# Adding routed-expert rows by accumulating DMAs: gathers into resident tokens for 30 tiles, scatters into the output for 9

## The chip, the core and the metric

The kernel runs on one core of one Trainium2 chip. The metric is the device time of one execution in microseconds (us), lower is better. The engines that matter here are TensorE (PE, matmuls; PEld is its weight load), VectorE (DVE), ScalarE (ACT), GpSimd (POOL), which issues the indirect DMAs, and SyncE (SP), which issues most plain DMAs. They run unsynchronised and wait on semaphores; a DMA adds 16 to its semaphore when it has landed.

## The reference

A decoder block over x of 4 x 512 tokens, 256 wide: a state-space mixer, a cross-attention over 1601 context rows, and a mixture of 8 experts of which each token takes two. Only the last is touched by the change:

```python
x = x + mixer(layernorm(x))
x = x + cross_attention(layernorm(x), ctx, mask)
xt = layernorm(x)                                    # 2048 tokens x 256
scores = xt @ Wg.T                                   # 8 experts
topk_scores, topk_idx = top_k(scores, 2)
gate = silu(einsum('td,ehd->teh', xt, W1));  up = einsum('td,ehd->teh', xt, W2)
y = einsum('teh,edh->ted', gate * up, W3)            # hidden width 704
w = einsum('tke,tk->te', onehot(topk_idx), topk_scores)
out = x + einsum('te,ted->td', w, y)
```

## The kernel before

Two phases follow each other, each one block of five engine programs. `mixer_phase` computes mixer and attention; the residual stream `x_all` (16 groups of 128 tokens) stays in SBUF, and SP stores the normalised tokens to DRAM as `xn3_dram` (L306; the trace calls it `xn_dram`). At its start it also writes zeros over the DRAM tensor `ffn_sorted` (L270), with a source that lies in `yg`.

`routed_ffn_phase` sorts the token-expert pairs by expert. Each expert's pairs are padded to whole tiles of 128 rows, NT = 39 tiles in all. DVE's routing chain (L1278 to L1361) finds the two experts of each token, the place of each pair (`pos_f`, then `pos`: for each token its lower and its higher place), and, through one-hot tables and 32 small matmuls (L1447), the token of each place (`tok_id`). `first` and `w_low` put the two weights in the order of the places. POOL then gathers the 39 tiles of tokens from DRAM (L1180).

The tiles run in order of the experts. For tile i TensorE transposes the tokens, makes gate and up (`gate_up`, L1478), transposes the hidden rows (L1487, L1491) and multiplies by W3 (`down`, L1503); each product is three matmuls over a high and a low part of the operands. The steps are staggered: `gate_up` of tile i + 1 stands before `down` of tile i. DVE takes from each tile `rest_of_hidden`, `rest_of_tokens`, `multiply` and `evacuate` (L1388), which copies the result from PSUM to `y_sb`; SP stores it to `ffn_sorted` (L1109) and loads tokens of tile i + 4 into `tok_in` (L1104). POOL also loads and splits the weights of experts 2 to 7 (L1151, L1154).

The end: when the stores of all experts but the last are there, POOL gathers for each token its row at the lower place into `y_one`, 16 gathers (L1195); when all 39 tiles are stored, the 16 rows at the higher places, into the space of `tok`. DVE adds each with its weight (L1425, L1430) and SP stores two groups at a time to the output (L1132):

```python
for p in range(2):
    pool.wait_ge(y_st[p], so_far(NT - 1 if (NT - 1) % 2 == p else NT - 2, p))
fetch(y_two, 1, lambda g: up_ld[g // 2])
...
nc.vector.scalar_tensor_tensor(out=x_all[:, g, :], in0=y_two[:, g, :], scalar=w_low[:, 1, g:g + 1],
                               in1=x_all[:, g, :], op0=ALU.mult, op1=ALU.add).then_inc(comb, 1)
```

Of the kernel before, what the change touches and what calls it, by code (L numbers as in the profile page):

```python
# [17 lines left out]
NEG_HUGE = -3.0e38  # L18


def at(i, n=1):
    return bass.ds(i, n)
# [9 lines left out]
def decoder_kernel(nc, io, dims):  # L32
    B, S, D, S2, DI, NST, TAPS, E, HF = dims
    KD = D // P
    KI = DI // P
    T = S // P
    G = B * T
    KC = -(-S2 // P)
    S2_LAST = S2 - (KC - 1) * P
    CH = -(-S2 // 4)  # L40
    CHUNKS = [(c * CH, min(S2, (c + 1) * CH)) for c in range(4)]
    KH = -(-HF // P)
    H_LAST = HF - (KH - 1) * P
    HH = HF // 2
    NT = (2 * B * S + E * (P - 1)) // P

    ffn_sorted = nc.dram_tensor("ffn_sorted", [NT * P, D], F32).ap()
    xn3_dram = nc.dram_tensor("xn3_dram", [G * P, D], F32).ap()
# [42 lines left out]
def mixer_phase(nc, io, dims, env, sem, buf):  # L91
# [9 lines left out]
    xn3_dram, b_dram, NT = (env[k] for k in ("xn3_dram", "b_dram", "NT"))  # L101
# [7 lines left out]
    with ExitStack() as ctx:  # L109
# [3 lines left out]
        def ps(name):  # L113
# [50 lines left out]
        zeros, ones, bo_row = yg[:, 0, 0:D], yg[:, 1, 0:P], yg[0:1, 2, 0:D]  # L164
# [12 lines left out]
            sem(n) for n in ("x_ld", "xr_ld", "wi_ld", "w_ld", "wa_ld", "b_st", "b_ld", "ctx_ld", "mask_ld", "tok_st", "res_st"))  # L177

# [70 lines left out]
        with nc.Block() as block:  # L249

            @block.sync
            def _(sp):
# [5 lines left out]
                for dst, src in (  # L258
# [44 lines left out]
                def store_tokens(b):  # L303
                    for t in range(T):
                        sp.wait_ge(LN[2]["xn"], b * T + t + 1)
                        sp.dma_start(xn3_dram[at(b * S + t * P, P), :], xn[:, t, :]).then_inc(tok_st, 16)  # L306
# [7 lines left out]
                for b in range(B):  # L314

                    if b >= 1:
                        load_mask(b - 1, 2)
                        load_mask(b - 1, 3)
                    if b + 1 < B:
                        store_b(b + 1)  # L320
                        load_b(b + 1, 0)
                        load_b(b + 1, 1)
                    if b >= 1:
                        context(b)
                        load_mask(b, 0)
                        load_mask(b, 1)
                    if b + 1 < B:
                        load_b(b + 1, 2)
                        load_b(b + 1, 3)
                    if b >= 1:  # L330
                        store_tokens(b - 1)
                load_mask(B - 1, 2)
# [209 lines left out]
            def _(dve):  # L542
# [42 lines left out]
                def read_out(b, j):  # L585
# [5 lines left out]
                    if isinstance(b, int) and b == 0 and j == 0:  # L591
                        dve.wait_ge(res_st, 16)
                        dve.wait_ge(res_st, 16)
# [372 lines left out]
def routed_ffn_phase(nc, io, dims, env, sem, buf):  # L966
# [5 lines left out]
    KD, G, KH, H_LAST, HH, NT = (env[k] for k in ("KD", "G", "KH", "H_LAST", "HH", "NT"))  # L972
# [8 lines left out]
    with ExitStack() as ctx:  # L981
# [8 lines left out]
        tok = sb("tok", [P, NT, D])  # L990
# [21 lines left out]
        first = sb("first", [P, 2, G])  # L1012
        w_low = sb("w_low", [P, 2, G])
# [19 lines left out]
        y_one = sb("y_one", [P, G, D])  # L1033
        y_two = tok[:, 0:G, :]

# [35 lines left out]
        low_ld, up_ld, comb = sem("low_ld"), [sem(f"up_ld{g}") for g in range(G // 2)], sem("comb")  # L1071
# [21 lines left out]
        with nc.Block() as block:  # L1093

            @block.sync
            def _(sp):
# [3 lines left out]
                def load(i, q):  # L1100

                    come = gathered(i) if isinstance(i, int) else (i - q) * (16 // PAIRS) + 32
                    sp.wait_ge(tok_ld[q // 2], come)
                    sp.dma_start(tok_in[:, q % 2, :], tok[:, at(i), :].rearrange("p a d -> p (a d)")  # L1104
                                 ).then_inc(tile_ld[q % 2], 16)
# [15 lines left out]
                LAST = (NT - AHEAD) // GROUP * GROUP  # L1121
# [14 lines left out]
            def _(pool):  # L1136
                nc.gpsimd.iota(iot[:], pattern=[[1, P]], base=0, channel_multiplier=0).then_inc(iota_ok, 1)
                nc.gpsimd.iota(num[:], pattern=[[P, G]], base=0, channel_multiplier=1).then_inc(iota_ok, 1)
# [4 lines left out]
                nc.gpsimd.memset(seg[:, :, 0:1], 0.0).then_inc(one_ok, 1)  # L1143

# [48 lines left out]
                def fetch(y, k, done):  # L1193
                    for g in range(G):
                        pool.indirect_dma_start(y[:, g, :], None, ffn_sorted,  # L1195
                                                bass.IndirectOffsetOnAxis(ap=pos[:, k, g:g + 1], axis=0)).then_inc(done(g), 16)
# [63 lines left out]
            def _(dve):  # L1260
# [59 lines left out]
                chain(nc.vector.tensor_tensor(first[:, 0, :], pos_f[:, 0, :], pos_f[:, 1, :], ALU.is_lt))  # L1320
                chain(nc.vector.tensor_scalar(first[:, 1, :], first[:, 0, :], -1.0, 1.0, ALU.mult, ALU.add))
# [3 lines left out]
                nc.vector.tensor_copy(pos[:], pos_f[:]).then_inc(pos_ok2, 1)  # L1325


# [75 lines left out]
                def pair(i):  # L1403
                    for k in range(2):
                        rest_of_hidden(i + k - 1)
                        rest_of_tokens(i + k + 1, k)
                        multiply(i + k, 1 - k)
                        evacuate(i + k - 1, k)

                pair(1)  # L1410
                with dve.Fori(3, NT - 2, 2) as i:
                    pair(i)
                rest_of_hidden(NT - 3)
                rest_of_tokens(NT - 1, 0)
                multiply(NT - 2, 1)
                evacuate(NT - 3, 0)
                rest_of_hidden(NT - 2)
                multiply(NT - 1, 0)
                evacuate(NT - 2, 1)
                rest_of_hidden(NT - 1)  # L1420
                evacuate(NT - 1, 0)

                dve.wait_ge(low_ld, 16 * G)
                for g in range(G):
                    nc.vector.scalar_tensor_tensor(out=x_all[:, g, :], in0=y_one[:, g, :], scalar=w_low[:, 0, g:g + 1],  # L1425
                                                   in1=x_all[:, g, :], op0=ALU.mult, op1=ALU.add).then_inc(comb, 1)
                for g in range(G):
                    dve.wait_ge(comb, g + 1)
                    dve.wait_ge(up_ld[g // 2], 32)
                    nc.vector.scalar_tensor_tensor(out=x_all[:, g, :], in0=y_two[:, g, :], scalar=w_low[:, 1, g:g + 1],  # L1430
                                                   in1=x_all[:, g, :], op0=ALU.mult, op1=ALU.add).then_inc(comb, 1)
# [150 lines left out]
```

## Time and profile before

| what | value |
|---|---|
| median of 3 runs | 1149.94 us |
| the runs | 1152.03, 1149.91, 1149.94 us |
| the profiled execution, first to last instruction | 1151.0 us |
| mean granted TensorE clock, as a share of full speed | 0.885 |
| busy share of PE, PEld, DVE, ACT, POOL | 81%, 64%, 58%, 39%, 51% |

The profile is of one execution. Its own device time is not listed apart from its span of 1151.0 us, which lies between the lowest and the highest of the runs. The second phase begins at 788.94 us of the span. A row of the timeline gives start, duration, engine, line, operation, what it writes and reads, and in brackets how long its engine was idle before and what ended that. A row of the chain of waits gives start, duration and what the chain went through.

### The profile page before, as it was taken

What the parts mean: (1) busy time and instruction counts of PE and PEld (TensorE: products, weight loads), DVE (VectorE), ACT (ScalarE), POOL (GpSimd) and SP (SyncE); (2) the same over time, 40 slices, a digit from 0 to 9 for tenths busy, and PEclk for the clock granted to TensorE, in tenths of its full rate; (3) what the DMA queues carried; (4) which work ended last, traced back from release to release, by engine and by line L of the source; (5) the groups of instructions that cost most, each with busy time, mean ns of one, the idle gap of its engine ahead of it and who ended that gap; (6) DMA issues with size and microseconds to landing.
All of it is one profiled execution on the core that took longest, in us unless ns stands there. A gap on an engine that the chain in (4) does not pass through costs nothing. (4 is left out here: it accounts for less than half of the span.)

```text
span 1151.0 us, 16215 instructions
## 1 busy us (share of the span) xinstructions
PE 928.8 (81%) x5148; PEld 731.9 (64%) x5149; DVE 669.2 (58%) x1097; ACT 445.6 (39%) x827; POOL 590.9 (51%) x481
## 2 busy tenths in 40 slices
PE   5767677889877889885989877992699999999970
PEld 2344345457666546665657765672689899999970
DVE  4189777697457788547677872416634343443443
ACT  2455754355544445635345530322222222222210
POOL 2176675755446565546576743110578553335505
PEclk9869877899886899996899987995699999999995
DMA  9440030000044000026000040004365312311304
GB/s 322 161 175 1 1 111 37 1 15 1 1 163 132 1 9 7 1 75 220 1 8 8 1 147 1 15 1 169 123 207 127 125 48 100 112 36 36 109 19 146
DMA packets 48954, 85.44 MB, mean 74 GB/s; under 512 B 6292, under 2 KB 38696, under 8 KB 46856
## 3 DMA queue, kind: packets, MB, share of 16 engines
q1 hardware_dynamic: 43032, 65.77, 17.0%
q0 software_dynamic: 5872, 19.02, 5.7%
q8 instruction: 29, 0.48, 0.2%
q14 instruction: 21, 0.17, 0.0%
HBM read 65.64 MB, written 14.55 MB: 70 GB/s over the span
## 5 line engine op out<-in xcount | busy, mean ns | idle before, releaser
L373 POOL TENSOR_TENSOR u<-dtx,b_all 128x512 f32<-128x512 f32 x256 | 326.6, 1288 | 212.9 <-DVE h L620 209.7
L620 DVE TENSOR_TENSOR_SCAN h<-da,u 128x512 f32<-128x512 f32 x256 | 308.6, 1217 | 136.8 <-ACT da L455 89.5
L455 ACT ACTIVATE da<-dt_,a_neg 128x512 f32<-128x512 f32 x256 | 174.8, 689 | 133.3 <-DVE h L620 132.5
L746 PE MATMUL ysum<-ident,h 128*128 128x128 f32 x1024 | 159.3, 301 | 57.9 <-DVE h L620 44.5
L746 PEld LDWEIGHTS ysum<-ident,h 128*128 128x128 f32 x1024 | 132.5, 156 | 104.2 <-DVE h L620 56.8
L924 PE MATMUL pv<-pT,ctx_n 128*128 128x128 f32 (+1 forms) x832 | 109.5, 288 | 7.6 <-DVE x_all L681 7.6
L924 PEld LDWEIGHTS pv<-pT,ctx_n 128*128 128x128 f32 (+1 forms) x832 | 104.6, 204 | 10.8 <-DVE x_all L681 9.1
L895 PE MATMUL pa<-ctx_t,xnT_a 128*128 128x401 f32 (+1 forms) x256 | 97.3, 508 | 13.9 <-DVE sim L602 12.6
L1367 DVE TENSOR_TENSOR hid<-act_,ps_u 128x352 f32<-128x352 f32 x78 | 40.6, 521 | 86.8 <-ACT act_ L1221 86.8
L1221 ACT ACTIVATE act_<-ps_g 128x352 f32<-128x352 f32 x78 | 36.3, 466 | 104.2 <-PE ps_u L1478 104.2
L1503 PE MATMUL ps_y<-w_hi,hidT_hi 128*128 x234 | 70.9, 303 | 2.7 <-DVE hidT_lo L1381 2.7
L895 PEld LDWEIGHTS pa<-ctx_t,xnT_a 128*128 128x128 f32 x256 | 44.9, 192 | 44.2 <-DVE sim L602 19.2
L729 PE MATMUL pm<-xnT_m,w_in 128*128 128x512 f32 x128 | 65.1, 637 | 6.3 <-DVE xs L576 4.8
L1503 PE MATMUL ps_y<-w_lo,hidT_hi 128*128 x234 | 66.5, 284 | 0.0
L1503 PE MATMUL ps_y<-w_hi,hidT_lo 128*128 x234 | 66.3, 283 | 0.0
L1226 ACT CAST hidT_hi<-ps_h 128x512 fp32r<-128x512 f32 x39 | 22.9, 586 | 104.3 <-PE ps_h L1491 100.1
L1180 POOL DMA_INDIRECT tok<-xn_dram,tok_id x39 | 43.9, 1125 | 35.3 <-DVE tok_id L1349 23.7
L1381 DVE TENSOR_TENSOR hidT_lo<-ps_h,hidT_hi 128x512 fp32r<-128x512 f32 (+2 forms) x117 | 42.1, 415 | 34.1 <-ACT hidT_hi L1226 34.1
L602 DVE COPY_PREDICATED sim<-mask,pa 128x401 f32<-128x401 uint8 x64 | 38.0, 596 | 37.1 <-PE pa L895 37.1
L1154 POOL TENSOR_TENSOR w_lo<-w_raw,w_hi 128x2816 fp32r<-128x2816 f32 (+1 forms) x12 | 58.6, 4882 | 0.0
L1478 PE MATMUL ps_g<-w_hi,tokT_hi 128*128 x156 | 54.6, 350 | 3.4 <-issue 3.3
L1162 POOL TENSOR_TENSOR pool_scrap<-ident 128x1 f32<-128x1 f32 x26 | 4.8, 193 | 96.3 <-PE ps_y L1503 85.3
(216 smaller groups left out, 1780.5 us busy)
## 6 DMA issues: line engine op xcount, KB each, us to landing
b_all<-b_dram SPq DMA_DIRECT2D x16, 1024.0 KB, 4.6
ctx_t<-in_ctxT SPq DMA_DIRECT2D x4, 1601.0 KB
ctx_n<-in_ctx SPq DMA_DIRECT2D x4, 1536.0 KB
ffn_sorted<-yg SPq DMA_DIRECT2D x1, 4992.0 KB, 22.5
ffn_sorted<-y_sb SPq DMA_DIRECT2D x39, 128.0 KB
tok_in<-tok SPq DMA_DIRECT2D x35, 128.0 KB, 2.0
mask<-in_mask SPq DMA_DIRECT2D x16, 200.1 KB, 2.4
w_raw<-in_w1T SPq DMA_DIRECT2D x4, 704.0 KB, 4.2
```

The source lines that it names most:

```text
L373: nc.gpsimd.tensor_tensor(u[:, i % 2, :], dtx[:, j % 2, :], b_all[:, n, :], ALU.mult).then_inc(u_ok, 1)
L455: nc.scalar.activation(da[i % DS][:], dt_[:, j % 2, :], ACT.Exp, scale=a_neg[:, j, n:n + 1]).then_inc(da_ok, 1)
L620: nc.vector.tensor_tensor_scan(h[:, i % HS, :], da[i % DS][:], u[:, i % 2, :], 0.0, ALU.mult, ALU.add).then_inc(scan_ok, 1)
L729: last = nc.tensor.matmul(bank[:], w_in[:, k, j * P:(j + 1) * P], xnT_m[:, k, :], start=k == 0, stop=k == KD - 1)
L746: last = nc.tensor.matmul(ysum[:, t * P:(t + 1) * P], h[:, i % HS, t * P:(t + 1) * P], ident[:], is_transpose=True, start=n == 0 and t == ...
L895: last = nc.tensor.matmul(pa[c % 2][:, 0:hi - lo], xnT_a[:, k, q * P:(q + 1) * P], ctx_t[:, k, lo:hi], start=k == 0, stop=k == KD - 1)
L924: last = nc.tensor.matmul(pv[:, k * P:(k + 1) * P], ctx_n[0:w, c, k * P:(k + 1) * P], pT[0:w, c, :], start=c == 0 and k == 0, stop=c == KC ...
L1154: nc.gpsimd.tensor_tensor(w_lo[:, p * NW + lo:p * NW + hi], w_raw[:, p, lo:hi], w_hi[:, p * NW + lo:p * NW + hi].bitcast(F32), ALU.subtrac ...
L1180: pool.indirect_dma_start(tok[:, i, :], None, xn3_dram, bass.IndirectOffsetOnAxis(ap=tok_id[:, i:i + 1], axis=0)).then_inc(tok_ld[i // 2 % ...
L1381: nc.vector.tensor_tensor(hidT_lo[0:rows_in, c:c + n, :], bank[0:rows_in, col:col + n * P].rearrange("p (c m) -> p c m", m=P), hidT_hi[0:r ...
L1478: last = nc.tensor.matmul(out[:, 0:HH], x[:, p, k * P:(k + 1) * P], w[:, at(e % 2 * NW + (first + k * HF), HH)], start=k == 0 and n == 0, ...
L1503: last = nc.tensor.matmul(ps_y[:, 0:D], x[0:rows_in, c, :], w[0:rows_in, at(e % 2 * NW + (2 * NGU + c * D), D)], start=c == 0 and n == 0, ...
```

## The change

A row's weight is applied when its tile is evacuated. For that the scores travel with the tokens: `xn3_dram` and `tok` have rows of 256 + 8 numbers, row 0 of `xn3_dram` is zero and belongs to empty places, and four stores write the scores. From them DVE works out one weight per row of each tile (`tile_masks`, `row_weights`).

The results of tiles 0 to 29 go to `ffn_sorted` as before. When tile 29 is stored, POOL adds them to `x_all` with 32 gathers that accumulate in SBUF; a place in a later tile points at a row of zeros. SP then stores `x_all` to the output. The results of tiles 30 to 38 stay in SBUF (`y_late`), and after SP's stores POOL adds them to the output in DRAM with 17 scatters that accumulate: 8 for rows that are their token's lower place, 9 for the higher, with waits between, so that no two additions to a row are in flight together. Rows that a scatter is not to add go to spare rows behind the output (`late_rows` works out where). The DVE additions at the end, `y_one`, `first` and `w_low` are gone. DVE's loop over pairs of tiles is written out.

```diff
-                sp.dma_start(env["ffn_sorted"].rearrange("(n p) d -> p n d", p=P),
-                             zeros.unsqueeze(1).to_broadcast([P, NT, D])).then_inc(res_st, 16)
+                sp.dma_start(env["ffn_sorted"][EARLY * P:(EARLY + 1) * P, :], zeros[:, 0:D]).then_inc(res_st, 16)
+                sp.dma_start(xn3_dram[0:1, :], zeros[0:1, :]).then_inc(res_st, 16)
...
+                def store_scores(b):
+                    sp.wait_ge(r_ok, b + 1)
+                    sp.dma_start(xn3_dram[at(b * S + 1, S), D:D + E].rearrange("(t p) e -> p t e", p=P),
+                                 scores[:, b * T:(b + 1) * T, :]).then_inc(score_st, 16)
...
+                store_scores(B - 1)
                 sp.wait_ge(tok_st, 16 * B * T)
+                sp.wait_ge(score_st, 16 * B)
...
+        BATCHES = [range(LATE - 3)] + [range(t, t + 1) for t in range(LATE - 3, LATE - 1)]
...
-                for i in range(LAST, NT - AHEAD):
+                for i in range(LAST, EARLY):
                     store_and_load(i, i % GROUP)
-                for i in range(NT - AHEAD, NT):
-                    store(i, i % 2)
-                out = io["out"].rearrange("(g p) d -> p g d", p=P)
+                for i in range(EARLY, NT - AHEAD):
+                    sp.wait_ge(y_ok2, i + 1)
+                    load(i + AHEAD, (i + AHEAD) % GROUP)
+                out = io["out"][0:G * P, :].rearrange("(g p) d -> p g d", p=P)
                 for g in range(0, G, 2):
-                    sp.wait_ge(comb, G + g + 2)
+                    sp.wait_ge(both_ld[g // 2], 64)
                     sp.dma_start(out[:, g:g + 2, :], x_all[:, g:g + 2, :]).then_inc(out_st, 16)
...
+                nc.gpsimd.memset(above[:], 1.0).then_inc(above_one, 1)
+                pool.wait_ge(above_one, 1)
+                nc.gpsimd.memset(above[:, :, E:E + 1], 0.0).then_inc(above_one, 1)
...
+                def add_early(k, g):
+                    pool.indirect_dma_start(x_all[:, g, :], None, ffn_sorted,
+                                            bass.IndirectOffsetOnAxis(ap=pos[:, k, g:g + 1], axis=0),
+                                            compute_op=ALU.add).then_inc(both_ld[g // 2], 16)
+
+                def add_late(k, t, done):
+                    pool.wait_ge(y_ok2, EARLY + t + 1)
+                    pool.indirect_dma_start(io["out"], bass.IndirectOffsetOnAxis(ap=late_to[:, k, t:t + 1], axis=0),
+                                            y_late[:, t, :], None, compute_op=ALU.add).then_inc(done, 16)
...
                 for p in range(2):
-                    stores = pool.value_load(tile_end[0:1, E + p:E + p + 1], min_val=1, max_val=NT)
-                    pool.wait_ge(y_st[p], stores * 16)
-                    take_wait()
-                fetch(y_one, 0, lambda g: low_ld)
-
-                for p in range(2):
-                    pool.wait_ge(y_st[p], so_far(NT - 1 if (NT - 1) % 2 == p else NT - 2, p))
-                fetch(y_two, 1, lambda g: up_ld[g // 2])
+                    pool.wait_ge(y_st[p], so_far(EARLY - 1 if (EARLY - 1) % 2 == p else EARLY - 2, p))
+                for g in range(G):
+                    add_early(0, g)
+                for g in range(G):
+                    pool.wait_ge(both_ld[g // 2], 32)
+                    add_early(1, g)
+
+                pool.wait_ge(late_ok, 1)
+                pool.wait_ge(out_st, 16 * (G // 2))
+                for n, batch in enumerate(BATCHES):
+                    for t in batch:
+                        add_late(0, t, low_st[n])
+                    if n == 0:
+                        pool.wait_ge(low_st[0], 16 * len(BATCHES[0]))
+                    else:
+                        pool.wait_ge(low_st[n - 1], 16 * len(BATCHES[n - 1]))
+                    for t in batch:
+                        add_late(1, t, high_st)
+                pool.wait_ge(low_st[len(BATCHES) - 1], 16)
+                add_late(1, LATE - 1, high_st)
+                pool.wait_ge(high_st, 16 * LATE)
...
-                chain(nc.vector.tensor_tensor(first[:, 0, :], pos_f[:, 0, :], pos_f[:, 1, :], ALU.is_lt))
-                chain(nc.vector.tensor_scalar(first[:, 1, :], first[:, 0, :], -1.0, 1.0, ALU.mult, ALU.add))
...
-                nc.vector.tensor_copy(pos[:], pos_f[:]).then_inc(pos_ok2, 1)
...
                 for k in range(2):
-                    chain(nc.vector.tensor_tensor(w_part[:, 0, :], w_top[:, 0, :], first[:, k, :], ALU.mult))
-                    chain(nc.vector.tensor_tensor(w_part[:, 1, :], w_top[:, 1, :], first[:, 1 - k, :], ALU.mult))
-                    chain(nc.vector.tensor_tensor(w_low[:, k, :], w_part[:, 0, :], w_part[:, 1, :], ALU.add))
+                    chain(nc.vector.tensor_scalar(is_late[:, k, :], pos_f[:, k, :], float(EARLY * P), None, ALU.is_ge))
+                    chain(nc.vector.tensor_scalar(to_zero[:, k, :], pos_f[:, k, :], num_f[:, 0:1], float(EARLY * P - 1),
+                                                  ALU.subtract, ALU.subtract))
+                    chain(nc.vector.tensor_tensor(to_zero[:, k, :], to_zero[:, k, :], is_late[:, k, :], ALU.mult))
+                    chain(nc.vector.tensor_tensor(pos_f[:, k, :], pos_f[:, k, :], to_zero[:, k, :], ALU.subtract))
+                nc.vector.tensor_copy(pos[:], pos_f[:]).then_inc(pos_ok2, 1)
...
                 def evacuate(i, p):
                     dve.wait_ge(y_mm, i + 1)
-                    wait(dve, y_st[p], so_far(i - 2, p))
-                    nc.vector.tensor_copy(y_sb[:, p, :], ps_y[:, 0:D]).then_inc(y_ok2, 1)
+                    if i < EARLY:
+                        wait(dve, y_st[p], so_far(i - 2, p))
+                    y = y_sb[:, p, :] if i < EARLY else y_late[:, i - EARLY, :]
+                    nc.vector.tensor_scalar(y, ps_y[:, 0:D], w_row[:, i:i + 1], None, ALU.mult).then_inc(y_ok2, 1)
...
+                rest_of_hidden(0)
+                rest_of_tokens(2, 0)
+                multiply(1, 1)
+                tile_masks()
+                row_weights(0, KNOWN)
+                for i in range(NT):
+                    if i > 0:
+                        rest_of_hidden(i)
+                        if i + 2 < NT:
+                            rest_of_tokens(i + 2, i % 2)
+                        if i + 1 < NT:
+                            multiply(i + 1, (i + 1) % 2)
+                    if i == KNOWN:
+                        row_weights(KNOWN, NT)
+                    if i == KNOWN + 1:
+                        late_rows()
+                    evacuate(i, i % 2)
```

`KNOWN` is 8. `tile_masks` is two DVE operations, `row_weights` two with a wait for the gathers of its tiles, and `late_rows` some twenty, on at most 9 x 8 numbers a partition.

## Rows read from the trace of the kernel before

**Rows 1.** The page: the span, and busy tenths of PE in 40 slices.
```profile
span 1151.0 us, 16215 instructions
PE   5767677889877889885989877992699999999970
```
**Rows 2.** The chain of waits, from the last tile's matmuls to the end.
```profile
1114.36 3.92 PE ps_y L1503 x18
...
1118.31 0.44 DVE y_sb L1388
...
1120.72 1.22 POOL tok L1195
...
1142.60 2.85 DMA tok<-ffn_sorted,pos
```
**Rows 3.** Timeline of POOL: last weight split, last lower gather, second higher gather.
```profile
1050.88 3.51 POOL L1154 TENSOR_TENSOR w_lo<-w_raw,w_hi 128x1536 fp32r<-128x1536 f32 x1
...
1084.33 0.96 POOL L1195 DMA_INDIRECT y_one<-ffn_sorted,pos  x1 [0.30 <-issue]
...
1122.24 3.65 POOL L1195 DMA_INDIRECT tok<-ffn_sorted,pos  x1 [0.30 <-issue]
```
**Rows 4.** The chain of waits: `down` of tiles 29 and 35.
```profile
1051.90 2.34 PE ps_y L1503 x18
...
1095.02 2.34 PE ps_y L1503 x18
```
**Rows 5.** Timeline of POOL: plain loads of 640 rows and of 64.
```profile
885.65 0.91 POOL L1079 DMA_DIRECT2D w_raw<-in_w3T  x1
886.52 0.63 POOL L1081 DMA_DIRECT2D w_raw<-in_w3T  x1
```
**Rows 6.** DMA queues from 1064 to 1086 us, POOL's: packets, MB, share of 16 engines.
```profile
q0 software_dynamic: 721, 1.97, 32.7%
```
**Rows 7.** DMA issues: count, KB each, median us from issue to landing.
```profile
out<-x_all SPq DMA_DIRECT2D x8, 256.0 KB, 2.3
...
xn_dram<-xn SPq DMA_DIRECT2D x16, 128.0 KB, 3.9
...
b_dram<-sp_pos SPq DMA_DIRECT2D x4, 32.0 KB, 1.6
```
**Rows 8.** Timeline of DVE at the end: the lower additions, the last higher pair.
```profile
1118.65 6.41 DVE L1425 SCALAR_TENSOR_TENSOR x_all<-y_one,w_low,x_all 128x256 f32<-128x256 f32 x16
...
1145.54 0.88 DVE L1430 SCALAR_TENSOR_TENSOR x_all<-tok,w_low,x_all 128x256 f32<-128x256 f32 x2 [1.66 <-DMA tok<-ffn_sorted,pos]
```
**Rows 9.** Token gathers as one group (min/median/max ns, first to last start); DVE beside them.
```profile
L1180 POOL DMA_INDIRECT tok<-xn_dram,tok_id x39: 956/960/4835, 813.9 to 868.4; - x39
...
815.90 4.74 DVE L1394 TENSOR_TENSOR w_lo<-w_raw,w_hi 128x2816 fp32r<-128x2816 f32 x2
```
**Rows 10.** Timeline where the phases meet; then the rank matmuls.
```profile
788.47 0.19 DVE L692 COPY scores<-pv 128x32 f32<-128x32 f32 x1 [5.68 <-PE pv L942]
788.94 0.38 SPq L1077 DMA_DIRECT2D w_raw<-in_w1T  x1
...
789.86 0.35 POOL L1146 TENSOR_SCALAR_AFFINE_SELECT tri<-tri 128x128 f32<-128x128 f32 x1
...
794.89 0.80 PE ps_g L1439 x2
```
**Rows 11.** The chain of waits: a routing step, the second half of the table matmuls.
```profile
800.93 0.19 DVE first L1320
...
809.77 3.59 PE ps_y L1447 x16
```
**Rows 12.** Timeline of DVE: evacuations of tile 0 and of a late tile.
```profile
838.34 0.42 DVE L1388 COPY y_sb<-ps_y 128x256 f32<-128x256 f32 x1 [1.76 <-PE ps_y L1503]
...
1083.13 0.42 DVE L1388 COPY y_sb<-ps_y 128x256 f32<-128x256 f32 x1 [1.44 <-PE ps_y L1503]
```
**Rows 13.** Timeline near the start: the clearing store, TensorE's wait for a load.
```profile
11.40 3.55 SPq L270 DMA_DIRECT2D ffn_sorted<-yg  x1
11.94 0.50 PEld L729 LDWEIGHTS pm<-xnT_m,w_in 128*128 128x128 f32 x2 [1.18 <-DMA b_conv<-in_b_conv]
```

More of the change, by code:

```diff
@@ L18 @@
 NEG_HUGE = -3.0e38
+OUT_OF_WAY = 1.0e30
+LATE = 9
 def at(i, n=1):
@@ L100, in mixer_phase @@
     x_all, ident, scores = env["x_all"], env["ident"], env["scores"]
-    xn3_dram, b_dram, NT = (env[k] for k in ("xn3_dram", "b_dram", "NT"))
+    xn3_dram, b_dram, EARLY = (env[k] for k in ("xn3_dram", "b_dram", "EARLY"))
     STEPS = KI * NST
@@ L163, in mixer_phase @@
         b_qkv = sb("b_qkv", [P, 3, KD])
-        zeros, ones, bo_row = yg[:, 0, 0:D], yg[:, 1, 0:P], yg[0:1, 2, 0:D]
+        zeros, ones, bo_row = yg[:, 0, 0:D + E], yg[:, 1, 0:P], yg[0:1, 2, 0:D]
         ysum = ps("ysum")
@@ L331, in _ @@
                         store_tokens(b - 1)
+                        store_scores(b - 1)
                 load_mask(B - 1, 2)
@@ L1032, in routed_ffn_phase @@
         tile_expert = sb("tile_expert", [1, LOOP], I32)
-        y_one = sb("y_one", [P, G, D])
-        y_two = tok[:, 0:G, :]
+        y_late = sb("y_late", [P, LATE, D])
+        above = sb("above", [P, NT, E + 1])
+        w_tile = sb("w_tile", [P, NT, E])
+        w_row = sb("w_row", [P, NT])
+        low_s = sb("low_s", [P, LATE, E])
+        high_s = sb("high_s", [P, LATE, E])
+        low_max = sb("low_max", [P, LATE])
+        high_max = sb("high_max", [P, LATE])
+        row_id = sb("row_id", [P, LATE])
+        taken_by = sb("taken_by", [P, 2, LATE])
+        dump = sb("dump", [P, 2, LATE])
+        away = sb("away", [P, 2, LATE])
+        late_to = sb("late_to", [P, 2, LATE], U32)
+        is_late = sb("is_late", [P, 2, G])
+        to_zero = sb("to_zero", [P, 2, G])
         place_row = w_lo[:, NW:NW + 2 * G * P].rearrange("p (k g m) -> p k g m", k=2, g=G)
@@ L1070, in routed_ffn_phase @@
                              "y_ok2"))
-        low_ld, up_ld, comb = sem("low_ld"), [sem(f"up_ld{g}") for g in range(G // 2)], sem("comb")
+        both_ld = [sem(f"both_ld{g}") for g in range(G // 2)]
+        above_one, w_row_ok, late_ok = sem("above_one"), sem("w_row_ok"), sem("late_ok")
+        BATCHES = [range(LATE - 3)] + [range(t, t + 1) for t in range(LATE - 3, LATE - 1)]
+        low_st, high_st = [sem(f"low_st{n}") for n in range(len(BATCHES))], sem("high_st")
+        KNOWN = 8
         def load_expert(eng, e, p, done):
@@ new lines, in row_weights, with late_rows @@
+                def row_weights(lo, hi):
+                    for n in range(PAIRS):
+                        last = max(i for i in range(hi) if i // 2 % PAIRS == n)
+                        dve.wait_ge(tok_ld[n], gathered(last))
+                    chain(nc.vector.tensor_tensor(w_tile[:, lo:hi, :], w_tile[:, lo:hi, :], tok[:, lo:hi, D:D + E], ALU.mult))
+                    chain(nc.vector.reduce_sum(w_row[:, lo:hi], w_tile[:, lo:hi, :], AX_X))
+                def late_rows():
+                    own, late = tok[:, EARLY:NT, D:D + E], above[:, EARLY:NT, :]
+                    chain(nc.vector.tensor_scalar(low_s[:], late[:, :, 1:E + 1], OUT_OF_WAY, -OUT_OF_WAY, ALU.mult, ALU.add))
+                    chain(nc.vector.tensor_tensor(low_s[:], low_s[:], own, ALU.add))
+                    chain(nc.vector.scalar_tensor_tensor(out=high_s[:], in0=late[:, :, 0:E], scalar=-OUT_OF_WAY, in1=own,
+                                                         op0=ALU.mult, op1=ALU.add))
+                    chain(nc.vector.reduce_max(low_max[:], low_s[:], AX_X))
+                    chain(nc.vector.reduce_max(high_max[:], high_s[:], AX_X))
+                    chain(nc.vector.tensor_copy(row_id[:], tok_id[:, EARLY:NT]))
+                    chain(nc.vector.tensor_scalar(taken_by[:, 0, :], row_id[:], 1.0, None, ALU.is_ge))
+                    chain(nc.vector.tensor_tensor(taken_by[:, 1, :], low_max[:], high_max[:], ALU.is_ge))
+                    chain(nc.vector.tensor_tensor(taken_by[:, 1, :], taken_by[:, 1, :], taken_by[:, 0, :], ALU.mult))
+                    chain(nc.vector.tensor_tensor(taken_by[:, 0, :], taken_by[:, 0, :], taken_by[:, 1, :], ALU.subtract))
+                    for k in range(2):
+                        chain(nc.vector.tensor_scalar(dump[:, k, :], num_f[:, 0:LATE], float((G + k * LATE) * P - 1), None, ALU.add))
+                        chain(nc.vector.scalar_tensor_tensor(out=away[:, k, :], in0=row_id[:], scalar=-1.0, in1=dump[:, k, :],
+                                                             op0=ALU.add, op1=ALU.subtract))
+                    chain(nc.vector.tensor_tensor(away[:], away[:], taken_by[:], ALU.mult))
+                    chain(nc.vector.tensor_tensor(away[:], away[:], dump[:], ALU.add))
+                    nc.vector.tensor_copy(late_to[:], away[:]).then_inc(late_ok, 1)
@@ L1401, in _ @@
                 split_rest(1)
[L1403 to L1431, printed above, removed]
+                rest_of_hidden(0)
[15 more added lines that the diff above has]
+                    evacuate(i, i % 2)
             @block.tensor
```

37 lines of the change are left out of this document (19 added, 18 removed).

## The prediction

> **What bounds the kernel now.** I read the page first: TensorE (PE) is busy nine tenths or more in every slice from the 30th to the 38th, then 7 and 0 [rows 1]. So the end is set by two things in turn, TensorE and what follows it. The chain of waits shows them: the matmuls of the last tile end at 1118.28 us, DVE evacuates them, SP stores them, POOL wakes at 1120.72 and issues sixteen gathers, the last at 1142.60, which lands 2.85 later [rows 2]. VectorE (DVE) adds the last pair, SyncE (SP) stores it: the tail is 1151.0 - 1118.3 = 32.7 us in which TensorE does nothing. The timeline of POOL shows what is idle before: the last expert's split ends at 1054.4, the last of the 16 gathers of the lower rows ends at 1085.3, beside the matmuls, and then POOL waits until 1120.72 [rows 2, 3]. One gather follows the other in 0.96 busy + 0.30 = 1.26 us. Six tiles lie between the two `down` groups of [rows 4], 43.12 us, so a tile takes TensorE 7.19; they are those of tile 29, which ends at 1054.24, and of tile 35, at 1097.36.
>
> **The tail, part by part.** The change takes away the wait for all tiles before the second set, the 32 DVE additions, and the output stores at the end. It adds 17 accumulating scatters (8 lower tiles, 9 higher), so POOL has 32 + 17 = 49 indirect DMAs on one chain in place of 32, of which 16 lay beside matmuls. No row shows an accumulating DMA. Its issue is bounded below by the plain one, 1.26 us from start to start, and above by twice the busy time, 2 x 0.96 + 0.30 = 2.22 us, if every row needs all of its descriptor work twice. Between them, plain DMAs of POOL show what more rows cost: 0.63 us with 64 rows, 0.91 with 640 [rows 5], so 0.28/576 = 0.5 ns a row, 0.07 us for 128 more rows. An accumulating DMA reads one more row per row, so I take 1.26 + 0.07 = 1.33 us. On the DMA engines the 16 gathers of rows 3 took 32.7% of the engines over 22 us, 0.45 us each [rows 6]; with a second read twice that, 0.90 us, which is under 1.33 and so hides behind the issue, but I add 0.5 us to each landing that the chain waits for: 2.85 + 0.5 = 3.35 us.
>
> The Trainium skill (Collectives: The Full Stack, section The bandwidth ceiling) says that an add in a DMA is slow not for the add but because it reads two sources, with two read descriptors per chunk on one ring, about half the rate. That agrees with the doubling that I used for the transfer, 0.90 us; read as a rule for the issue too, it would give the 2.22 us of the first rival.
>
> The chain then, in times of the trace before:
> - POOL starts 2.44 us after tile 29's matmuls, as it did after tile 38's (1118.28 to 1120.72) [rows 2]: 1056.7. It is free of the split by 1054.4 [rows 3].
> - 31 starts of 1.33: 1097.9; landing 3.35: 1101.3. The waits for the lower rows of a pair cost nothing: they landed some 15 issues before.
> - SP stores the last pair, 2.3 us [rows 7]: 1103.7 with 0.1 of hand-over; POOL wakes after 0.3: 1104.0. SP's queue has the loads of tiles up to 38 ahead of these stores, the last of them after tile 34's evacuation at 1090.6; the stores of the first pairs stand behind it, but the last pair comes 10 us later, so 0.
> - Six lower scatters, last start after 5 x 1.33: 1110.6; landing 3.35 and 0.3: 1114.3. Tile 35 was ready at 1098.
> - Six higher, lower 6, higher 6, then lower 7 starts at + 8 x 1.33 (counted from the first higher): 1124.9; it lands and POOL wakes: 1128.6; the last scatter lands at 1131.9.
> - From the last landing to the end of the span before: the last output store starts after the DVE pair that ends at 1146.42, lands 2.3 later, at 1148.7, and 2.3 us remain [rows 7, 8]. So 1134.2.
>
> The last tile's rows are there at 1118.3 + 0.5 and are asked for at 1128.6: TensorE has 9 us of slack against POOL in the new order. In this chain 31 + 5 + 8 = 44 issue times count.
>
> DVE's 16 additions, back to back from 1118.65 for 6.41 us, also go. Beside them POOL's second gather took 3.65 us instead of 0.96 [rows 3, 8], and the longest token gather took 4.83 us beside DVE's two-input subtractions of 4.74 [rows 9]. This stall is in the old tail alone; next to the short DVE work of the tiles the 16 gathers stayed at 0.96, so I add none.
>
> **The start of the second phase.** The mixer's last act is now a store of the last scores. The scores are copied at 788.47 + 0.19, and the next phase began at 788.94 [rows 10], with no DMA between. Now SP waits for 512 pieces of 32 bytes: a 32 KB store took 1.6 us to land, the token stores 3.9 [rows 7]; I take 2.2, since these bytes are few but the pieces small. The score stores of the other three batches stand in SP's queue behind the token stores of their batch and ahead of the mask loads of the next, which wait for later attention steps: 0.
>
> The Trainium skill (DMA: Bandwidth & Descriptors, Specifications) says that under 512 bytes a transfer becomes a read-modify-write; no row here shows it. By that rule the upper end would be the nearer.
>
> In the routing chain the two `first` steps and the conversion of `pos`, 0.2 us each with their hand-over, go from ahead of the one-hot tables: -0.6. Behind the tables, six weight steps go and nine small ones come, 9 x 0.2 = 1.9 us; TensorE's 16 matmuls of 3.59 us cover them, as nothing waits for DVE before they end [rows 11]. Without that cover they would cost 1.9. POOL's two more memsets lie ahead of the triangle, which is ready at 790.2 and needed at 794.89 [rows 10]: 0, even at the 0.35 us of the triangle's own operation each. The gathers carry 1056 bytes for 1024, 3% of 0.45 us under an issue of 1.26: 0. Sum of this part: +2.2 - 0.6 = +1.6 (bounds +1.0 and +3.3).
>
> **Inside the tiles.** The weighted evacuation is one operation from PSUM for another, 0.42 us [rows 12]: 0. The two mask steps and the first two weight steps, four times 0.2 to 0.4, lie between multiply 1 and evacuation 0, where DVE waited 1.76 us. The second weight steps wait for all 39 gathers: the last started at 868.42 [rows 9], and tile 8 is evacuated 8 x 7.19 us after tile 0 (838.34), near 896. `late_rows`, some 20 steps of 0.2 = 4 us, comes before evacuation 9: DVE has 1.44 us of idle there [rows 12] and more behind it, 7.19 us a tile against some 3.5 of work, so the tile absorbs most; 0, at worst 2.5, and even that lies in the 9 us of slack, save for tile 29, from which POOL starts. DVE's tile loop is now written out; if its code comes late, it eats the same 1.44 us.
>
> **The start of the kernel.** The 4992 KB clearing store is cut to 128 KB. The only wait of TensorE for a load near it, 1.18 us for `b_conv`, ended at 11.94, half a microsecond after that store was issued, so it was due to earlier transfers [rows 13]: 0, at most -1.2.
>
> **Sum.** 1134.2 + 1.6 = 1135.8 against a span of 1151.0: -15.2 us. The median of the runs is 1149.94, 1.1 under that span, so 1134.7; I say 1135.
>
> **Rivals.**
> - The plain price holds: 1.26 us and a landing of 2.85. Then 44 x 0.07 + 4 x 0.5 = 5.1 us less: 1129.6. The 16 gathers beside the matmuls speak for it; that they read one source speaks against. It belongs to the forecast's own case, as does an issue up to 1.60 (+12: 1147).
> - The accumulating issue costs POOL twice: 2.22 us. Then 44 x 0.89 = 39 us more: 1174, slower. It decides from 1.33 + 15.2/44 = 1.68 us on, a busy time of 1.38 against 0.96. For it: the indirect DMA's 0.96 against 0.63 for a plain one says that work per row matters. Against it: 0.5 ns a row for the plain ones.
> - The DMA engines become the bound: read, read and write of a row in sequence, four times 0.45 = 1.8 us per DMA. The rings fill and the chain goes at 1.8: 44 x 0.47 = 21 us more, 1156, slower. For it: 1 KB rows; against: the gathers of rows 6 kept the engines busy for only a third of the time.
> - The change does not help because POOL's chain is simply moved: the start of the adds waits for something later than tile 29. Each tile of delay costs 7.2 us, so two give 1149, no change. No row speaks for it; the stores and the split end before.
>
> **How the numbers follow.** Forecast with an issue of 1.26 to 1.60: 0.68, its own range 1129 to 1147. POOL twice: 0.14. DMA engines: 0.11. Delayed start: 0.07. The range must leave out no more than 2 in 10: it goes from 1128 to 1158, which takes in the second slower case, and leaves out the first. This measurement can tell about 0.2%, 2.3 us. Faster: 0.68 and half of the delayed start, 0.71; same: 0.04; slower: 0.25.
>
> **What the profile after would show.** POOL's busy time for one accumulating DMA (0.96, 1.03 or 1.9) is the first thing to read; then the start of the first (1058), the start of the first scatter (1105), the last (1130), and TensorE's last matmul at 1118.3 + 1.6 = 1119.9. Wrong would be: a busy time above 1.38, landings beyond 5 us, or a second phase that begins later than 793.

## The result and the profile after

The changed kernel takes 1165.12 us (median of 4 runs, 1163.73 to 1167.2) against 1149.93 for the kernel before: ratio 1.013, 95% interval 1.0114 to 1.0147. It is 15 us slower where 15 us less were forecast. The profiled execution, the run of 1163.73, spans 1162.0 us.

The chain of waits of the changed kernel, its last part (answers to rows 2):

```profile
1113.09 1.56 POOL x_all L1224
1114.64 5.56 issue
1120.20 1.60 POOL out L1230
...
1129.57 3.76 DMA out<-y_late,late_to
1133.33 0.45 issue
1133.78 1.55 POOL out L1230
...
1148.63 3.75 DMA out<-y_late,late_to
1152.38 0.27 issue
1152.64 1.55 POOL out L1230
```

The whole end is now POOL and its landings. The gap of 5.56 us is the landing of the last gather, SP's last output store and its landing. TensorE has ended long before; the timeline of DVE shows the evacuation of its last tile, which starts 37 us ahead of the last scatter:

```profile
1115.63 0.48 DVE L1435 TENSOR_SCALAR y_late<-ps_y,w_row 128x256 f32<-128x256 f32 x1 [3.98 <-PE ps_y L1573]
```

The two kinds of accumulating DMA of the changed kernel, grouped by the tile they write (duration in ns min/median/max, first and last start, us); the plain one before took 0.96 us [rows 3]:

```profile
L1224 POOL DMA_INDIRECT x_all<-ffn_sorted,pos x32: 1548/1557/1712, 1055.2 to 1113.1; - x32
```
```profile
L1230 POOL DMA_INDIRECT out<-y_late,late_to x17: 1551/1552/1599, 1120.2 to 1152.6; - x17
```

The first gather, in the timeline of POOL, where the chain of the additions begins:

```profile
1055.19 1.71 POOL L1224 DMA_INDIRECT x_all<-ffn_sorted,pos  x1 [2.96 <-DMA ffn_sorted<-y_sb]
```

Busy 1.56 and 0.30 to the next make 1.86 us from start to start. The starts give (1113.09 - 1055.19)/31 = 1.87, as a few gathers took up to 1.71. On the DMA engines, from 1056 to 1114 us, POOL's queue (packets, MB, share of 16 engines) took 49.9% of 58 us for 31 gathers, 0.93 us each, where plain ones took 0.45 [rows 6]:

```profile
q0 software_dynamic: 4377, 3.99, 49.9%
```

So the transfer is twice as costly, as assumed, and hidden: POOL starts a gather every 1.87 us. What was put too low is the time of POOL itself. At the phases' border (timeline, answers to rows 10) SP now waits for its store of the scores:

```profile
787.68 0.19 DVE L703 COPY scores<-pv 128x32 f32<-128x32 f32 x1 [5.68 <-PE pv L953]
787.90 0.37 SPq L314 DMA_DIRECT2D xn_dram<-scores  x1
790.13 0.38 SPq L1102 DMA_DIRECT2D w_raw<-in_w1T  x1
```

From the end of the copy, 787.87, to the next phase it is 2.26 us; before it was 0.28.

### The profile page after: what moved, and what is told of

It reads as the page before. It is cut to its first block and busy times, and to the rows that moved or that the text cites. A ratio compares the mean times of both kernels' runs of the same rounds, so it can differ in the third digit from the quotient of the medians.

```text
span 1162.0 us, 15965 instructions
## 1 busy us (share of the span) xinstructions
PE 925.7 (80%) x5148; PEld 727.0 (63%) x5149; DVE 668.0 (57%) x1088; ACT 445.6 (38%) x827; POOL 634.3 (55%) x498
## 5 line engine op out<-in xcount | busy, mean ns | idle before, releaser
L740 PE MATMUL pm<-xnT_m,w_in 128*128 128x512 f32 x128 | 67.9, 660 | 6.4 <-DVE xs L588 4.3
L1209 POOL DMA_INDIRECT tok<-xn_dram,tok_id x39 | 44.3, 1136 | 34.5 <-DVE tok_id L1394 22.9
L1224 POOL DMA_INDIRECT x_all<-ffn_sorted,pos x32 | 50.0, 1562 | 12.4 <-issue 9.5
```

The source lines that it names most:

```text
L740: last = nc.tensor.matmul(bank[:], w_in[:, k, j * P:(j + 1) * P], xnT_m[:, k, :], start=k == 0, stop=k == KD - 1)
L1209: pool.indirect_dma_start(tok[:, i, :], None, xn3_dram, bass.IndirectOffsetOnAxis(ap=tok_id[:, i:i + 1], axis=0)).then_inc(tok_ld[i // 2 % ...
L1224: pool.indirect_dma_start(x_all[:, g, :], None, ffn_sorted, bass.IndirectOffsetOnAxis(ap=pos[:, k, g:g + 1], axis=0), compute_op=ALU.add). ...
```

## The experiments

Twelve kernels ran, in three groups; each group has its own runs of the kernel before beside it (median 1151.22, 1150.85 and 1151.93 us), and ratios are to those. e1 to e4 and e10 leave out or misplace part of the additions, so their output is not the reference's; e2, e3 and e10 ran once each, and are read by their traces.

**Is it the accumulating form, and of which DMAs?** In e1 the early gathers lose `compute_op`, in e4 the scatters do:

```diff
-                                            bass.IndirectOffsetOnAxis(ap=pos[:, k, g:g + 1], axis=0),
-                                            compute_op=ALU.add).then_inc(both_ld[g // 2], 16)
+                                            bass.IndirectOffsetOnAxis(ap=pos[:, k, g:g + 1], axis=0)).then_inc(both_ld[g // 2], 16)
```

> The 32 early gathers do not accumulate: they overwrite x_all, so the added rows replace the residual and the output is not the reference's. Theory A (accumulating costs POOL more for every DMA, 1.86 us from start to start in place of 1.26): the gathers go back to 1.26 us, the chain from the first gather to the out store is 31 x 0.60 = 18.6 us shorter and the landing about 1 us, so about 1145.5 us. Rival (the extra 27 us against the forecast lie mostly in waits and at the end, not in the issue): less than 10 us shorter, above 1155.

> The 17 late scatters overwrite the output rows instead of adding (the output is not the reference's). Theory A: their busy time goes from 1.55 to 0.96 us, 16 issues on the chain are 9.6 us shorter, the landings they wait for about 1 us each: about 1153 us. Rival: a scatter into DRAM costs more than a gather whether it adds or not, busy stays above 1.3: above 1160.

e1: 1147.34 us, ratio 0.9961 (0.9946 to 0.9975), 18 us under the changed kernel. e4: 1154.41 us, ratio 1.0035 (1.0021 to 1.0049), 11 us under it. The groups by tile, of e1:

```profile
L1224 POOL DMA_INDIRECT x_all<-ffn_sorted,pos x32: 945/949/1039, 1058.0 to 1097.0; - x32
```

and of e4:

```profile
L1230 POOL DMA_INDIRECT out<-y_late,late_to x17: 956/961/1048, 1122.8 to 1144.9; - x17
```

Gather or scatter, the plain form costs 0.95 to 0.96 us and the accumulating one 1.55 to 1.56. A scatter into DRAM is not dearer in itself, so e4's rival falls, and so does e1's. Together the two account for some 29 us, the shorter landings included: twice the loss.

**POOL's work or the DMA engines?** e2 halves the bytes of a row (first diff), e3 the rows (second):

```diff
-                    pool.indirect_dma_start(x_all[:, g, :], None, ffn_sorted,
+                    pool.indirect_dma_start(x_all[:, g, 0:D // 2], None, ffn_sorted.rearrange("n (h d) -> (n h) d", h=2),
```
```diff
-                    pool.indirect_dma_start(x_all[:, g, :], None, ffn_sorted,
-                                            bass.IndirectOffsetOnAxis(ap=pos[:, k, g:g + 1], axis=0),
+                    pool.indirect_dma_start(x_all[0:P // 2, g, :], None, ffn_sorted,
+                                            bass.IndirectOffsetOnAxis(ap=pos[0:P // 2, k, g:g + 1], axis=0),
```

> The 32 early accumulating gathers move 512 bytes a row in place of 1024, of other rows, 128 rows as before (the output is not the reference's). Theory A (POOL's work goes by rows): busy time stays at 1.55 us, the time at about 1165. Rival B (the DMA engines, which read two sources and write one, are the bound and hold POOL back): busy time falls clearly, towards 0.96, and the time by up to 18 us.

> The 32 early accumulating gathers take 64 rows in place of 128, of 1024 bytes (half of the tokens get no early rows). Theory A with all of the time per row: busy 0.78 us. Theory A with a fixed part like the 0.57 us at which a plain POOL DMA of 64 rows starts: busy 1.0 to 1.1 us. Rival B (bytes on the DMA engines): the same as in the run with half the bytes and all rows.

The gathers of e2, then of e3, grouped as above:

```profile
L1224 POOL DMA_INDIRECT x_all<-ffn_sorted,pos x32: 1548/1557/1711, 1057.1 to 1115.0; - x32
```
```profile
L1224 POOL DMA_INDIRECT x_all<-ffn_sorted,pos x32: 1419/1428/1591, 1055.1 to 1109.0; - x32
```

Half the bytes change nothing, 1.557 us; the time is 1164.74. On the DMA engines they did change something. POOL's queue, e2 from 1056 to 1110 us:

```profile
q0 software_dynamic: 3917, 1.79, 27.7%
```

That is 0.53 us for each of some 28 gathers in place of 0.93. So the DMA engines do not hold POOL back. Half the rows take 1.428 (e3, 1160.67 us), so a row costs 129/64 = 2.0 ns. If the time is a straight line over the rows, 1.30 us do not depend on them: more than either busy time that I had given for all of e3's DMA (0.78, 1.0 to 1.1). e10 halves the rows of e1's plain gathers (1146.12 us):

> The 32 early gathers plain and with 64 rows in place of 128 (output not the reference's). The accumulating gather took 1.56 us with 128 rows and 1.43 with 64: 2 ns a row and 1.30 us fixed. If the plain one has the same price per row, its busy time is 0.95 - 0.13 = 0.82 us and the accumulating form's extra 0.6 us is a fixed charge per DMA; if it has less than 1 ns a row (above 0.89), part of the extra goes by rows.

```profile
L1224 POOL DMA_INDIRECT x_all<-ffn_sorted,pos x32: 887/892/983, 1056.9 to 1094.1; - x32
```

A row of the plain form costs (949 - 892)/64 = 0.9 ns, and its fixed part, by the same straight line, is 0.83 us. Of the 0.61 us that accumulating adds per DMA of 128 rows, some 0.47 are fixed and 0.14 go by rows. The lines are drawn through two points each; no third number of rows was tried.

The queue also counts packets, and here the two forms differ. Divided by the bytes of one gather (128 KB, in e2 and e3 64 KB), a plain one has 48 packets (721 for 1.97 MB [rows 6]), an accumulating one 144 (4377 for 3.99 MB), and e2's, with all rows and half the bytes, 143. With 64 rows the accumulating one has 80; POOL's queue in e3, from 1056 to 1110 us:

```profile
q0 software_dynamic: 2468, 2.03, 27.6%
```

From 64 to 128 rows that is one packet a row for the accumulating form, and the plain one puts several rows into a packet. It may be why a row costs POOL more; that was not tried. It does not explain the fixed part: with 80 packets the accumulating DMA still takes 1.43 us, with 48 the plain one 0.95. What POOL does in these 0.47 us stays open.

**What follows the last landing.** In the changed kernel the last scatter starts at 1152.64 and lands some 3.8 later, at 1156.4; 5.6 us remain to the end of the span, where the kernel before had 2.3. e6 moves one line, from the end of POOL's program to the end of SP's:

```diff
+                sp.wait_ge(high_st, 16 * LATE)
...
-                pool.wait_ge(high_st, 16 * LATE)
```

> The changed kernel, but SP and not POOL waits for the landing of the last scatters. After the last landing (about 1156.4) the changed kernel still runs 5.6 us, the kernel before 2.3 us after its last landing. Theory C (POOL is slow to close its program after it has waited for its own DMA): POOL's closing then runs beside the landing, and the end comes 3 us sooner, about 1162 us. Rival D (the end of the block, or POOL's queue of DMAs, takes that long after the last accumulating scatter whoever waits): no change, 1165.

The scatters of e6, and the first line of its page:

```profile
L1231 POOL DMA_INDIRECT out<-y_late,late_to x17: 1550/1552/1599, 1123.9 to 1156.3; - x17
```
```profile
span 1163.2 us, 15965 instructions
```

From the last start to the end it is 6.9 us in place of 9.4, 2.5 us less: in the trace, part of what POOL still did after the landing now lies beside it. The time does not show it: 1164.88 us, ratio 1.0131 (1.0106 to 1.0156). In this execution the scatters began 3.7 us later than in the changed kernel's, for a part of the program that e6 does not touch. A gain of 2.5 us is within the interval, so whether the time gains it stays open, and with it rival D for the time.

**The parts that were costed at little.** e8 is the kernel before with the four score stores alone, e9 the kernel before with the clearing store cut to 8 tiles, e7 the kernel before with its lower additions (L1425), unchanged, moved between the steps of the last three tiles:

```diff
+                def add_low(groups):
+                    dve.wait_ge(low_ld, 16 * G)
+                    for g in groups:
...
                 evacuate(NT - 3, 0)
+                add_low(range(0, 5))
                 rest_of_hidden(NT - 2)
                 multiply(NT - 1, 0)
+                add_low(range(5, 8))
                 evacuate(NT - 2, 1)
+                add_low(range(8, 12))
                 rest_of_hidden(NT - 1)
+                add_low(range(12, 16))
                 evacuate(NT - 1, 0)
```

> The kernel before, with the four score stores of the change alone (to a DRAM tensor that nobody reads). The changed kernel's second phase began 2.26 us after SP issued the last of them was possible, in place of 0.28. Theory: +2.0 us, ratio 1.0017. Rival (the gap at the phases' border is hidden by POOL's and ScalarE's set-up): no change.

> The kernel before, with the clearing store cut from 39 tiles to the last 8 (4992 to 1024 KB). My forecast costed it at nothing: ratio 1.000. Rival: the changed kernel's first phase ended 0.8 us earlier (787.68 against 788.47), so the smaller store gives 0.8 us, ratio 0.9993.

> The kernel before, with the 16 additions of the lower rows moved from the end into the last three tiles of DVE's loop, nothing else. Theory E (DVE's additions back to back hold POOL's descriptor writing up: its second gather took 3.65 us instead of 0.96): the tail is 2.7 us shorter, ratio 0.9977. Rival (the second gather is slow for another reason, such as the first use after a pause): no change.

e8: ratio 1.0021 (1.001 to 1.0032), 2.4 us, near the 2.0 of its theory. e9: 0.9997 (0.9983 to 1.0011), which can't tell nothing from the 0.8 us of its rival. But the 0.8 us are no sign of the store: e9's own scores were copied at 789.12, later than the 788.47 before, and with the changed kernel's first phase the copy came anywhere from 786.69 (e4) to 789.15 (e6). e7: 1148.65 us, 0.9983 (0.9969 to 0.9996), 2 us faster. Its higher gathers, timeline of POOL:

```profile
1121.98 0.95 POOL L1195 DMA_INDIRECT tok<-ffn_sorted,pos  x1 [36.00 <-DMA ffn_sorted<-y_sb]
1123.23 0.95 POOL L1195 DMA_INDIRECT tok<-ffn_sorted,pos  x1 [0.30 <-issue]
```

The second takes 0.95 us where it took 3.65 [rows 3]: with the additions gone from beside it the delay is gone, and the pause ahead of the first gather, 36 us, is still there. So it was DVE's run of additions that held it, not a first use after a pause.

**Can the idea be had without the price?** h1 keeps the split at tile 30 and the scatters, but gathers plainly and lets DVE add, two groups at a time between the steps of tiles 31 to 36:

```diff
+        y_one, y_two = tok[:, G:2 * G, 0:D], tok[:, 0:G, 0:D]
...
+                def add_pair():
...
+                        nc.vector.tensor_tensor(x_all[:, g, :], x_all[:, g, :], (y_one, y_two)[k][:, g, :],
+                                                ALU.add).then_inc(comb, 1)
...
+                ADDS = {(EARLY + 1 + n // 3, n % 3) for n in range(G)}
```

> The changed kernel with its 32 early gathers plain, into the token buffer that is free by then, and the additions on DVE, two at a time, spread over the steps of tiles 31 to 36; the 17 scatters stay. Theory A (the price is the accumulating form's 0.60 us per DMA on POOL, and DVE has room): the first scatter starts at about 1101.4 in place of 1120.2, 18.8 us sooner: about 1146 us, ratio 0.9967. Rival F (32 more DVE additions delay TensorE or hold POOL's gathers up, as the 16 back to back did in the kernel before): first scatter after 1106, ratio 1.00 or more.

h1: 1148.38 us, ratio 0.9983 (0.9967 to 0.9998). The first scatter started at 1102.4, 17.8 us sooner than in the changed kernel, and the last tile was evacuated at 1115.9 against 1115.6 there, so rival F did not come. h2 has the scatters in another order, and DVE waits for four gathers at a time in place of two:

```diff
+ORDER = "L0 L1 L2 L3 L4 L5 H0 H1 H2 H3 L6 L7 H4 H5 H6 H7 H8"
...
+                        if t > 0:
+                            pool.wait_ge(low_st[t - 1], 16)
+                        add_late(1, t, high_st)
```

> The run before with the scatters in an order in which each finds the lower ones that it must follow landed: L0 to L5, H0 to H3, L6, L7, H4 to H8 (L lower, H higher, by late tile), each H waiting for one landing only. The waits of 2.66 and 0.30 us between the scatters go: 3 us less, about 1143 us, ratio 0.994. Rival G (landings of scatters to DRAM queue behind each other, so the waits come back at the H scatters): less than 1 us.

h2: 1147.79 us, 0.9972 (0.9959 to 0.9985). The first scatter started at 1103.8. The scatters of h2, grouped:

```profile
L1233 POOL DMA_INDIRECT out<-y_late,late_to x17: 1541/1548/1642, 1103.8 to 1133.5; - x17
```

29.7 us for 16 distances, 1.86 each: no wait is left in between, so rival G falls in the trace; the step in time, 0.6 us in the medians, is smaller than the 3 expected and inside both intervals. h3 changes several things at once: 5 tiles are scattered in place of 9, the lower gathers start when all experts but the last are stored, the additions lie in tiles 33 to 37, and SP waits for the last landing:

```diff
-LATE = 9
+LATE = 5
+ORDER = "L0 L1 H0 L2 H1 L3 H2 H3 H4"
...
+                    stores = pool.value_load(tile_end[0:1, E + p:E + p + 1], min_val=1, max_val=EARLY // 2)
+                    pool.wait_ge(y_st[p], stores * 16)
...
+                ADDS = {(33, 2): 2, (34, 0): 1, (34, 1): 1, (34, 2): 2, (35, 0): 1, (35, 1): 1, (35, 2): 1,
+                        (36, 0): 1, (36, 1): 1, (36, 2): 2, (37, 0): 3}
```

> The run before with only the last 5 tiles scattered (9 scatters in place of 17), the 16 lower gathers started when the tiles of all experts but the last are stored (as the kernel before does), the 16 higher ones after tile 33, the additions over tiles 33 to 37, and SP waiting for the last landing. By issue times of 1.26 and 1.86 the first scatter starts at about 1111, the last at 1126, the end is 1132.7 of the span: about 1136 us, ratio 0.988. Rival F: the DVE additions push TensorE's last tile beyond 1125, the last scatter waits for it: 1140 or more.

h3: 1142.2 us, ratio 0.9919 (0.9897 to 0.9941): faster than both kernels, by 9.7 us against the one before. How much of that each of its changes gave was not taken apart. The timeline, first of POOL and then of DVE, shows what it still loses against the expected 1136:

```profile
1087.79 1.21 POOL L1235 DMA_INDIRECT tok<-ffn_sorted,pos  x1 [0.79 <-DMA ffn_sorted<-y_sb]
...
1108.45 0.95 POOL L1235 DMA_INDIRECT tok<-ffn_sorted,pos  x1 [0.30 <-issue]
1118.84 1.64 POOL L1241 DMA_INDIRECT out<-y_late,late_to  x1 [9.44 <-issue]
```
```profile
1114.35 1.43 DVE L1509 TENSOR_TENSOR x_all<-x_all,tok 128x256 f32<-128x256 f32 x4 [4.70 <-DMA tok<-ffn_sorted,pos]
...
1124.82 0.48 DVE L1446 TENSOR_SCALAR y_late<-ps_y,w_row 128x256 f32<-128x256 f32 x1 [4.85 <-PE ps_y L1604]
```

The first scatter starts at 1118.8, not 1111: the higher gathers started at 1087.8, where four tiles of 7.16 us behind the changed kernel's 1055.2 would be 1083.8; some took 1.2 to 1.35 us beside DVE's additions, and the last, begun at 1108.45, let DVE on only at 1114.35, 5.9 us later. TensorE's last tile is ready at 1125.3, 9 us later than in the changed kernel: the first half of rival F came. It is asked for at 1133.8, so the second half, a last scatter that waits for it, did not.

## Why the prediction was wrong

The step that failed is the price of one accumulating issue, "so I take 1.26 + 0.07 = 1.33 us". It measured 1.86, and 1.87 in the mean of the chain. The chain from POOL's first gather to the end was forecast as 1134.2 - 1056.7 = 77.5 us and took 1162.0 - 1055.2 = 106.8. The 29.3 between them:

| term | forecast | measured | difference on the chain, us |
|---|---|---|---|
| issue, 44 on the chain | 1.33 | 1.87 | +23.6 |
| landing, four waited for | 3.35 | 3.75 to 3.9 | +1.8 |
| SP's last store with its two hand-overs | 2.7 | 3.2 | +0.5 |
| POOL's two wake-ups among the scatters | 0.3 each | 0.45, 0.26 | +0.1 |
| from the last landing to the end | 2.3 | 5.6 | +3.3 |
| sum | | | +29.3 |

The chain began 3.1 us earlier than forecast, which hides that much of the 29.3. The other way went the step from span to time: I took 1.1 us off the span, where the profiled run took 1.7 more than its own, 2.8 in all, and the median lies 1.4 above that run. So 29.3 - 3.1 + 2.8 + 1.4 = 30.4, from 1134.7 to 1165.1.

- The bounds for the issue, 1.26 and 2.22, held the value. The choice between them did not: I took the slope of plain DMAs over their rows (0.5 ns) for the whole extra. The form has a fixed price of its own, by the straight lines 0.47 us of the 0.61, which no row of the trace before could show (e3, e10), and its rows cost 2.0 ns against 0.9.
- My own point of decision was right: the change loses from 1.68 us an issue on, a busy time of 1.38. It measured 1.56. The rival that names POOL's issue is the one that came, at three fifths of its extra (23.6 of 39 us); 1174 was too much, and I gave it 0.14.
- The rival of the DMA engines as the bound fell: e2 moved half the bytes for the same 1.557 us. Its price was wrong too: a read, a read and a write, each as long as a whole plain DMA, would be three times 0.45 and not four, and it measured twice 0.45. The doubling for the transfer was right, 0.93 us against 0.90. The rule of the Trainium skill on two sources (Collectives: The Full Stack, section The bandwidth ceiling) agrees with the share of the queue, 0.45 to 0.93. For the issue, a plain doubling would have been nearer than my slope, 2.22 against 1.33 for 1.86, but e3 and e10 speak against it as the mechanism: most of the extra is there with half the rows.
- The end: the forecast took the 2.3 us of a kernel in which SP waited last, for a plain store. Where POOL waits last for its own accumulating scatter, the span ends 9.3 to 11.4 us after that scatter's start in the seven traces (9.4 in the changed kernel, 11.1 in e10, 11.4 in e3), and 6.9 us after it in the two where SP waits (e6, h3). The landing itself takes 3.7 to 3.8 of that. The traces show this; timed, the difference was not resolved, and what makes it range by 2 us is not known.
- The start of the second phase: right. The score store cost 2.26 - 0.28 = 2.0 us against 2.2 less the old gap, and 2.4 alone (e8). From the end of the scores' copy to the end of `tok_id` it was 26.65 us against 24.99 before, +1.7, where the sum said +1.6. The nine steps behind the tables had their cover.
- The tiles: right in sum, for a partly wrong reason. The second weight step took 3.8 us, not 0.4 (it waited for POOL, see the last section), and tile 8 came 2.4 us and tile 9 3.2 us later than before; by tile 10 it was 0.3, and tile 11 came earlier than before. Beyond that the tiles came earlier than forecast: POOL began at 1055.2 and not at 1058.3, with 7.16 us a tile instead of 7.19, and 0.9 and 1.3 us less ahead of tiles 11 and 16. In the seven executions with the same code up to there POOL began anywhere from 1055.1 to 1059.0, at 1057.0 in the mean, so over half of these 3 us is luck of this execution and no effect of the change.
- The start of the kernel: nothing speaks against the 0; e9 finds no difference, but could not have told one of 1.2 us.
- TensorE's slack was as said: its last result was ready 36 us before it was asked for, far more than 9, because POOL was later.

## What to carry to other kernels

An accumulating indirect DMA saves an addition that VectorE does in under half a microsecond (0.75 us for two in h1), mostly unseen, and pays 0.6 us more of POOL, which issues all of this kernel's indirect DMAs; where POOL's issues form the chain, gather plainly and add elsewhere, in pieces between other steps. Before moving a tail onto one engine's queue, count the issues in it: 49 times any unknown is a large number, and a form that the trace does not show needs a price of its own, not a slope from its neighbours. Splitting at a tile so that most of the tail runs beside the last matmuls was sound: with plain gathers, 9 scatters in place of 17 and an earlier start of the lower gathers it gave 0.8%.

## What the runs showed of the hardware

- POOL's busy time for one indirect DMA of n rows, worked out from 64 and 128 rows alone: about 0.83 us + 0.9 ns n for the plain form, 1.30 us + 2.0 ns n for the accumulating one. For the accumulating form it was the same for 512 and 1024 bytes a row, and for both forms, at 128 rows, the same for a gather into SBUF and a scatter into DRAM.
- An accumulating gather of 128 rows has 144 packets in POOL's queue, a plain one of the same rows 48.
- DVE and POOL hold each other up in both directions. DVE's additions back to back held one gather for 2.7 us, and it went away with them (e7). The other way round, DVE's product of 128x248 took 3.8 us while POOL subtracted 128x2816 numbers (timeline of the changed kernel):

```profile
893.92 6.25 POOL L1183 TENSOR_TENSOR w_lo<-w_raw,w_hi 128x2816 fp32r<-128x2816 f32 x1
...
896.63 3.81 DVE L1448 TENSOR_TENSOR w_tile<-w_tile,tok 128x248 f32<-128x248 f32 x1
```

That the company is the cause, other executions show, in which the same product started at another time against the same subtraction. In e1 it came when the subtraction was over (POOL's ended at 901.91) and took 0.41 us; in e4 it came 2.1 us before the subtraction's end at 901.29:

```profile
903.19 0.41 DVE L1447 TENSOR_TENSOR w_tile<-w_tile,tok 128x248 f32<-128x248 f32 x1
```
```profile
899.19 2.37 DVE L1448 TENSOR_TENSOR w_tile<-w_tile,tok 128x248 f32<-128x248 f32 x1
```

In all nine executions in which it started during the subtraction it ended 0.27 to 0.29 us after the subtraction's end, whether it had started 1.4 us before that (e10, 1.71 us long) or 3.5 (3.81 long). So DVE was held until POOL had finished, not slowed.
